# GpSimd adds all three projection tiles to the residual behind the mixing weights, ahead of the low half of the next x

## What is computed

```python
x = x + attention(group_norm(x))          # 32 groups
# attention(x):
q = conv1x1_bn(x, qw, ...)                 # 8 heads of 32
k = conv1x1_bn(x, kw, ...)
v4 = conv1x1_bn(x, vw, ...)                # 8 heads of 128
vl = depthwise_conv3x3(v4) * lv_s + lv_t
attn = einsum('bhid,bhjd->bhij', q, k) * SCALE + ab[:, BIAS_IDXS]
attn = softmax(einsum('bhij,gh->bgij', attn, th1w) + th1b)
attn = einsum('bhij,gh->bgij', attn, th2w) + th2b
o = relu(einsum('bhij,bhjd->bhid', attn, v) + vl)
return conv1x1_bn(o, pw, ...)              # back to 384 channels
```

## Time and profile before

| | |
|---|---|
| median of 3 runs | 4653.12 us (4652.32 to 4653.26) |
| the profiled execution: its time | 4652.12 us |
| the profiled execution: its span | 4650.3 us |
| TensorE busy (PE / PEld) | 4567.8 us (98%) / 4530.7 us (97%) |
| VectorE busy | 4405.2 us (95%) |
| ScalarE busy | 3370.8 us (72%) |
| GpSimd busy | 1128.9 us (24%) |
| DMA | 356 MB, 27.7% of the 16 engines' span |

### The profile page before, as it was taken

How to read it: one execution, slowest core, us unless ns; L and a number is a source line. 1 busy time by engine, 2 the same in 40 slices (tenths; PEclk the granted TensorE clock), 3 DMA queues, 4 the chain that set the end, 5 groups by cost and what they waited for, 6 DMA issues and landing times.

```text
span 4650.3 us, 108573 instructions
## 1 busy us (share of the span) xinstructions
PE 4567.8 (98%) x33794; PEld 4530.7 (97%) x33794; DVE 4405.2 (95%) x10833; ACT 3370.8 (72%) x7941; POOL 1128.9 (24%) x1093
## 2 busy tenths in 40 slices
PE   6999999999999999999999999999999999999999
PEld 6999999999999999999999999999999999999999
DVE  8999999999999999999999999999999999999998
ACT  5777777777777777777777777777777777777776
POOL 2222122122221222222212222122122221222212
PEclk9999999999999999999999999999999999999999
DMA  2223223222232232222322223223222232222322
GB/s 90 80 70 88 63 79 90 68 79 75 67 94 63 79 84 68 84 63 78 94 64 79 79 65 93 63 79 84 72 80 68 74 94 63 79 79 67 90 63 74
DMA packets 210781, 356.02 MB, mean 77 GB/s; under 512 B 15986, under 2 KB 132738, under 8 KB 210692
## 3 DMA queue, kind: packets, MB, share of 16 engines
q1 hardware_dynamic: 210756, 355.71, 27.7%
HBM read 199.67 MB, written 155.98 MB: 76 GB/s over the span
## 4 chain that ended last, share of the span: by engine, by line
PE 71%; issue 15%; DVE 13%; DVEq 0%; POOL 0%; DMA 0%; ACT 0%; POOLq 0%; SPq 0%
PE psA L288 38%; PE psA L423 11%; PE psM L288 10%; PE psL L288 10%; DVE psC L686 8%; DVE shared L686 2%; DVE probs L743 1%; DVE shared L785 1%; DVE nmax L743 0%; PE psA L306 0%; DVEq L680 0%; DVE rinv L764 0%; PE psA L301 0%; DVE q_lo L710 0%; DMA qa<-by_key 0%
## 5 line engine op out<-in xcount | busy, mean ns | idle before, releaser
L686 DVE SCALAR_TENSOR_TENSOR psC<-vpad,par,psC 128x406 f32<-128x406 f32 x3072 | 1795.4, 633 | 0.0
L561 ACT ACTIVATE probs<-probs,nmax 112x196 f32<-112x196 f32 x1792 | 799.5, 449 | 177.0 <-DVE nmax L743 168.7
L288 PE MATMUL psA<-x_hi,w_lo 128*128 128x392 f32 x2304 | 795.5, 345 | 8.5 <-DVE x_lo L667 8.5
L288 PE MATMUL psA<-x_lo,w_hi 128*128 128x392 f32 x2304 | 789.0, 342 | 0.0
L288 PE MATMUL psA<-x_hi,w_hi 128*128 128x392 f32 x2304 | 788.0, 342 | 0.0
L423 PE MATMUL psA<-qa,shared 105*128 105x196 f32 x4096 | 710.3, 332 | 50.4 <-DVE shared L785 49.3
L423 PEld LDWEIGHTS psA<-qa,shared 105*128 105x128 f32 x4096 | 677.8, 191 | 69.6 <-DVE shared L785 68.3
L710 DVE SCALAR_TENSOR_TENSOR q_lo<-qk,th,q_hi 128x392 fp32r<-128x392 f32 x1024 | 663.8, 677 | 0.0
L458 ACT ACTIVATE o_hi<-shared 128x392 fp32r<-128x392 f32 x512 | 264.8, 529 | 468.0 <-DVE shared L785 468.0
L466 ACT ACTIVATE q_hi<-qk,th 128x392 fp32r<-128x392 f32 x1024 | 595.6, 620 | 2.1
L840 POOL TENSOR_TENSOR k_lo<-qk,k_hi 128x392 fp32r<-128x392 f32 x128 | 168.0, 1312 | 1700.5 <-ACT k_hi L470 1700.5
(11 more groups left out here) (81 smaller groups left out, 10391.3 us busy)
## 6 DMA issues: line engine op xcount, KB each, us to landing
by_key<-probs SPq DMA_DIRECT2D x512, 224.0 KB, 3.8
qa<-by_key SPq DMA_DIRECT2D x128, 448.0 KB, 4.3
qk<-by_key SPq DMA_DIRECT2D x128, 448.0 KB, 6.9
xs<-in_x SPq DMA_DIRECT2D x64, 588.0 KB, 4.4
shared<-in_x SPq DMA_DIRECT2D x64, 588.0 KB, 3.8
out<-shared SPq DMA_DIRECT2D x63, 588.0 KB, 3.1
qa<-in_wqkv SPq DMA_DIRECT2D x3, 768.0 KB, 6.8
stage_wp<-in_wp SPq DMA_DIRECT2D x1, 1536.0 KB, 10.8
```

What stands on the lines that cost most here:

```text
L288: last = nc.tensor.matmul(dst, w, r, start=(begin and n == 0), stop=(end and n == 2))
L561: nc.scalar.activation(row, row, ACT.Exp, bias=nmax[:, img, b:b + 1], scale=-1.0, accum_out=rowsum[:, img, b:b + 1]).then_inc(s_exp, 1)
L686: nc.vector.scalar_tensor_tensor(a if tap == 7 else sums, src, taps[:, c, TAPS[tap]:TAPS[tap] + 1], a if tap == 0 else sums, MUL, ADD).the ...
```

## The change

The two additions m = 0 and 1 leave their place behind the low halves of the keys. All three additions now stand between the mixing weights and the low half of the next x; the wait for the load of `res` goes with them. Nothing else differs.

```diff
                     wait_alone(pool, s_khi, 2 * t + kt + 1)
                     nc.gpsimd.tensor_tensor(k_lo[:, kt, :], k[:, kt, :], k_hi[:, kt, :].bitcast(f32),
                                             SUB).then_inc(s_klo, 1)
-                if not first:
-                    pool.wait_ge(s_res, 16 * t)
-                    residual(t, 0)
-                    residual(t, 1)
                 if not last:
                     rstd(t + 1)
                     normalise(t + 1)
@@
                     pool.wait_ge(s_wphi, 1)
                     nc.gpsimd.tensor_tensor(wp_lo[:, :, :], stage_p, wp_hi[:, :, :].bitcast(f32), SUB).then_inc(s_wplo, 1)
                 if not first:
-                    residual(t, 2)
+                    pool.wait_ge(s_res, 16 * t)
+                    for m in range(CT):
+                        residual(t, m)
                 if not last:
                     pool.wait_ge(s_v_mm, VT * (t + 1))
                     if not first:
```

## The result

| | before | changed |
|---|---|---|
| median (runs) | 4652.72 us (6) | 4811.77 us (6) |
| lowest to highest | 4651.62 to 4653.68 | 4798.36 to 4832.22 |
| ratio, 95% interval | | 1.0347 (1.0315 to 1.0380) |
| profiled execution, its time / span | 4652.12 / 4650.3 us | 4831.7 / 4829.8 us |
| mean granted TensorE clock | 0.998 | 0.981 |

The change makes the kernel 3.5% slower. The direction and the place were forecast, the size was not: 4775 us were expected, with a range up to 4800. The runs spread over 34 us where the kernel before spreads over 2, and the profiled one is near the upper end.

What follows compares the result with a forecast made beforehand. VectorE's taps were taken to bound the last part of a step, TensorE the earlier part. 4652.12 us + 122.1 (62 loop steps x 1.97) + 1 for the last step = 4775 us; range 4650 to 4800.

Steps and rivals of the forecast that it cites:

- The path through a step: TensorE through values, projection and logits, VectorE from last scores through taps to first addition, TensorE from the third unit on.
- At 2099.68 three additions in a row, +1.97 us.: Behind the mixing weights: VectorE's first two-SBUF tap stands until all three additions end, +1.97 us in each of 62 loop steps.
- The rival of one instruction at a time: VectorE's tap gets in after the first addition, the second addition delays the second tap: +0.9 us a step, 4708 us, chance 0.13.
- I add nothing for the clock.: At TensorE's 2.6 us stop before the third unit, the granted clock stays at full level: nothing added.
- the rival where TensorE stops for over 5 us: `x_lo` asks before the second tap, which stands for its 2.69 us: +4.6 us a step, 4937 us or some 5100, chance 0.11.
- The gain ahead of the logits is worth 0.: VectorE gains 0.7 us on the low halves of the queries, but waits longer for logits at 2079.41: 0 a step.
- `x_lo` does not get in before the second tap.: Behind the three additions, the second two-SBUF tap asks 0.19 us before `x_lo` and goes first; `x_lo` waits some 0.4 us.
- The later store and loads are hidden.: The store starts 2 us later and the next x about 1 us later, but nothing arrives late.

Runs made afterwards that it cites:

- the filler: 20 unused TensorE products in the stop before the third attention-times-value unit: 4772.10 us on the changed kernel, 4755.81 us with its additions as one instruction.
- the merged instruction: The changed kernel with its three additions made one GpSimd instruction of 128x1176: 4865.74 us, ratio 1.0460 to the kernel before.
- with gaps: The changed kernel, where GpSimd waits for the end of each addition before starting the next: 4699.61 us, ratio 1.0101 to the kernel before.

## Why the prediction missed

*The path through a step.* Right. VectorE's taps set the end of a step behind the logits: the stop grew by exactly what the pair of taps grew by, 0.65 to 2.62 and 1.42 us, and taking 0.49 us from the pair took 0.49 us from the step.

*"At 2099.68 three additions in a row, +1.97 us."* Right in 41 of 61 steps, wrong in 20. The row that it went by, the tap that stood from `wp_lo` through `x_lo`, was one sample of something that goes both ways. The rival of one instruction at a time was priced at 0.9 and cost 0.77, and it holds in part of the steps of the same execution, which no case had foreseen. This took about 20 x 1.19 = 24 us off.

*"I add nothing for the clock."* This is the step that failed. The term was put at nothing. It rested on one window of the first step, in which TensorE was busy for 1.2 of 4.0 us and kept the full clock. Of the dear steps, 36 of 41 lost it, 79 us in the profiled execution. The row showed that TensorE can pause once without the clock falling, not that a stop of 2.6 us in each step leaves it up. The sum with both corrections is 4775 + 79 - 24 = 4830, against 4831.7 of that execution. And where the clock was kept by the filler, the same additions gave 4772, against the 4775 forecast. The lower clock was weighed only in the rival where TensorE stops for over 5 us, so the range ended at 4800.

*The gain ahead of the logits is worth 0.* Right in size, wrong in place: a wait for psL appeared at the third score (34.4 us in the span, where some 43 us were expected at psM), and the one for psM at 2079.41 did not grow. VectorE came to the third score just as its logits came, which the rows at 2076.32 and 2076.72 would have shown.

*`x_lo` does not get in before the second tap.* Right: no pair took over 3.66 us. *The later store and loads are hidden.* Right: the changed kernel with the filler, and the one with all additions behind the taps, leave nothing for them.

*The rule of the Trainium skill* ("SBUF — State Buffer", section "SBUF: two separate sides") of an exclusive lock for the whole instruction agrees with these traces: the merged instruction of 2.68 us holds VectorE's tap out in each of 61 steps, and with gaps the two engines alternate instruction by instruction in each of 61. What happens between two GpSimd instructions that are both ready varies here from step to step.

What stays open is what decides in a step of the changed kernel whether the tap gets in after the first addition. Apart from the first loop step, the tap asks 0.32 to 0.33 us behind the start of the first addition in both kinds. A gap of 0.27 us let it in in all 61 steps, one instruction in none, and with the filler it got in only in the first loop step, where it asks 0.55 us behind. The clock cannot be all of it: in the kernel with one addition moved both kinds occur at the full clock. What decides whether the clock falls is open too: the length of the stop is not enough, since 2.31 us lost it more often than 2.6 us. No kernel shifted the additions in small steps against the taps, which would be the next thing to try.

## What to carry to other kernels

Look at GpSimd's work by what VectorE runs beside it, not by its own time. In these kernels an addition of 1 us cost nothing beside a VectorE instruction with one SBUF input, and held one with two until it was over; a wait for the right VectorE instruction was worth more here than any earlier start. A stop on TensorE can cost about twice its length or more: 1.96 us more of it cost 3.64 or 5.16 us in the steps where the granted clock fell. So price a stop with and without that and let the range hold both. Time freed on an engine is worth something only in the part of the step where that engine is waited for.

## What was not expected of the hardware

The granted clock answers to differences of a stop that look too small to matter. Behind stops of 1.40 to 1.42 us it never fell, in 20 + 61 + 39 steps of three kernels; behind 1.62 us it fell in 13 of 22; behind 2.6 us in 36 of 41; behind 2.31 us, in the merged kernel, in all 61. So a longer stop did not always lose it more often; a dear step lost it more often when the step before was dear too. The fall comes around the end of the stop, 0.7 us before to 1.4 us after TensorE starts again in the changed kernel, and costs 1.7 us or 3.2 us each time, most of it while TensorE is already busy. Products whose results nobody uses, put into the stop, kept it up for 110 us of gain.
